# State scan of a two-direction GRU: three columns an image with prepared operands, in place of four

## The reference

```
def step(h, xt):
    gh = h @ whh.T + bhh
    xr, xz, xn = jnp.split(xt, 3, axis=-1)
    hr, hz, hn = jnp.split(gh, 3, axis=-1)
    r = jax.nn.sigmoid(xr + hr)
    z = jax.nn.sigmoid(xz + hz)
    n = jnp.tanh(xn + r * hn)
    h_new = (1.0 - z) * n + z * h
    return (h_new, h_new)
...
yf = _gru_dir(z @ gru_wih_f.T + gru_bih_f, gru_whh_f, gru_bhh_f, False)
yb = _gru_dir(z @ gru_wih_b.T + gru_bih_b, gru_whh_b, gru_bhh_b, True)
y = jnp.concatenate([yf, yb], axis=-1) @ out_w.T + out_b
return x + y.reshape(Bx, Hx, Wx, C)
```

## Time and profile before

| | us |
|---|---|
| median of 3 runs | 1848.66 |
| lowest, highest | 1848.02, 1849.30 |
| the profiled execution | 1848.42 |
| its span, from the first to the last instruction | 1846.6 |
| TensorE, VectorE, ScalarE busy | 1639.6, 1578.8, 1227.9 |

### The profile page before, as it was taken

The page is one execution under the profiler, slowest core; times in us unless marked ns, Lnnn a source line. Parts: engine busy times, 40 slices in busy tenths (PEclk is TensorE's granted clock), DMA queues, the critical chain, the costliest instruction groups (busy, mean ns, idle before and its releaser), DMA issues.

```text
span 1846.6 us, 65131 instructions
## 1 busy us (share of the span) xinstructions
PE 1639.6 (89%) x21315; PEld 1240.3 (67%) x21315; DVE 1578.8 (85%) x9056; ACT 1227.9 (66%) x6271; POOL 58.2 (3%) x131
## 2 busy tenths in 40 slices
PE   3558999999999999999999999999999999999997
PEld 2436777676777777777777777776777777777775
DVE  7879888888888888888888888888888888888887
ACT  7935666666666666666666666666666666666665
POOL 5520000000000000000000000000000000000000
PEclk9655555555555555555555555555555555555555
DMA  5200000000000000000000000000000000000000
GB/s 157 69 7 8 13 11 14 11 14 11 13 11 12 12 11 14 10 14 11 13 11 8 11 14 11 12 12 12 12 12 12 11 14 11 13 11 12 12 12 15
DMA packets 40132, 31.27 MB, mean 17 GB/s; under 512 B 3448, under 2 KB 37624, under 8 KB 39800
## 3 DMA queue, kind: packets, MB, share of 16 engines
q1 hardware_dynamic: 39800, 27.13, 5.1%
HBM read 18.73 MB, written 8.39 MB: 15 GB/s over the span
## 4 chain that ended last, share of the span: by engine, by line
PE 56%; DVE 22%; ACT 14%; issue 7%; DMA 0%; POOL 0%; SPq 0%; DVEq 0%; ACTq 0%; POOLq 0%
PE bank L592 56%; DVE state L888 8%; DVE bank L876 8%; ACT rec L496 7%; DVE halves L897 4%; ACT rpair L490 3%; ACT big L432 2%; ACT seq L428 1%; ACT xin L416 1%; DMA gamma_row<-in_gamma 0%; DVE seq L851 0%; DVE rec L903 0%; DVE big L867 0%; ACT zquad L493 0%; DVE xin L821 0%
## 5 line engine op out<-in xcount | busy, mean ns | idle before, releaser
L592 PEld LDWEIGHTS bank<-halves,wsplit 128*128 128x128 f16 x18432 | 697.8, 106 | 504.4 <-DVE halves L897 376.7
L592 PE MATMUL bank<-halves,wsplit 128*128 128x16 f16 x18432 | 883.6, 182 | 133.2 <-DVE halves L897 118.6
L888 DVE TENSOR_TENSOR_SCAN state<-zquad,rec 128x64 f32<-128x64 f32 x2048 | 596.2, 291 | 177.0 <-ACT rec L496 135.1
L592 PE MATMUL bank<-seq,wcomb 128*128 128x128 f32 x1536 | 593.0, 491 | 0.4 <-DVE seq L851 0.4
L496 ACT ACTIVATE rec<-bank 128x16 f32<-128x16 f32 x2048 | 406.5, 198 | 276.4 <-DVE bank L876 81.4
L490 ACT ACTIVATE rpair<-bank 128x16 f32<-128x16 f32 x2048 | 378.9, 185 | 285.7 <-PE bank L592 267.9
L897 DVE SCALAR_TENSOR_TENSOR halves<-state 128x32 f16<-128x32 f32 x2048 | 433.1, 211 | 34.8
L876 DVE TENSOR_TENSOR_SCAN bank<-rpair,bank 128x32 f32<-128x32 f32 x2048 | 440.5, 215 | 22.3 <-ACT rpair L490 6.2
L493 ACT ACTIVATE zquad<-bank 128x16 f32<-128x16 f32 x2048 | 407.6, 199 | 25.1
L592 PEld LDWEIGHTS bank<-seq,wcomb 128*128 128x128 f32 x1536 | 385.9, 312 | 1.3 <-DVE seq L851 1.3
L903 DVE TENSOR_TENSOR rec<-state,signs 128x32 f32<-128x32 f32 x2047 | 370.9, 181 | 3.0
(11 more groups left out here) (118 smaller groups left out, 204.8 us busy)
## 6 DMA issues: line engine op xcount, KB each, us to landing
xin<-in_x SPq DMA_DIRECT2D x16, 512.0 KB, 3.7
big<-in_x SPq DMA_DIRECT2D x128, 64.0 KB
out<-big SPq DMA_DIRECT2D x128, 64.0 KB
wih<-in_wiht SPq DMA_DIRECT2D x2, 384.0 KB
con<-in_consts SPq DMA_DIRECT2D x1, 424.0 KB, 5.3
whh<-in_whht SPq DMA_DIRECT2D x2, 192.0 KB
inw<-in_in_w SPq DMA_DIRECT2D x1, 128.0 KB
outw<-in_outwt SPq DMA_DIRECT2D x2, 64.0 KB
```

The costliest lines, as they stand in the source:

```text
L592: return nc.tensor.matmul(o, w, m, start=start, stop=True, skip_group_check=True)
L888: v.tensor_tensor_scan(state[:, d, ring, :], zquad[:, e, cols], rec[:, e, cols], 0.0, ALU.mult, ALU.add).then_inc(state_ready[d], 1)
```

## The change

The state scan has three columns an image. Its first operand, `gain`, holds 0, K * (1 - z), 1; its second, `drive`, holds -n, (1 - z - 1) * h, -BIG, and is subtracted. The columns become n, K * (1 - z) * n + z * h, which is the new state, and the new state + BIG. ScalarE writes 1 - z to a dense tile `keep` and tanh of the negated candidate to column 0 of `drive`. VectorE makes the middle columns: `scale_gain` multiplies `keep` by K into `gain`, and `hold_state` computes (`keep` - 1) * h, with the last state h, into `drive`. Both are of 16 columns. They stand in `body` where `record_state` stood, but belong to the state scan that follows them, of the same direction and step. `signs`, `rec`, `zquad` and `rec_ready` go; `gain_ready` and `drive_ready` come. The memsets of the start are 11 in place of 15. The split, the projection and `state_of` read every third column where they read every fourth.

```diff
--- before
+++ after
-    state = sb("state", [P, 2, RING + 1, 4 * B])
-    rec = sb("rec", [P, 2, 4 * COLS])
-    signs = sb("signs", [P, 2 * COLS])
+    state = sb("state", [P, 2, RING + 1, 3 * B])
+    drive = sb("drive", [P, 2, 3 * COLS])
-    zquad = sb("zquad", [P, 2, 4 * COLS])
+    keep = sb("keep", [P, 2, COLS])
+    gain = sb("gain", [P, 2, 3 * COLS])
...
                     act.wait_ge(update_pre[d], turn)
-                    act.activation(zquad[:, e, 4 * B * d:4 * B * (d + 1)].rearrange("p (n k) -> p n k", k=4)[:, :, 2],
+                    act.activation(keep[:, e, B * d:B * (d + 1)],
                                    Z[q][:, at:at + B], ACT.Sigmoid, scale=negative).then_inc(update_ready[d], 1)
                     act.wait_ge(cand_pre[d], turn)
-                    act.activation(rec[:, e, 4 * B * d:4 * B * (d + 1)].rearrange("p (n k) -> p n k", k=4)[:, :, 0],
+                    act.activation(thirds_of(drive, e, d)[:, :, 0],
...
-                                   ACT.Tanh, scale=inverse).then_inc(cand_ready[d], 1)
+                                   ACT.Tanh, scale=negative).then_inc(cand_ready[d], 1)
...
             dve.wait_ge(cand_ready[d], turn)
-            dve.wait_ge(update_ready[d], turn)
-            if not (isinstance(base, int) and base + r == 0):
-                dve.wait_ge(rec_ready[d], base + r)
-            v.tensor_tensor_scan(state[:, d, ring, :], zquad[:, e, cols], rec[:, e, cols], 0.0,
-                                 ALU.mult, ALU.add).then_inc(state_ready[d], 1)
+            dve.wait_ge(gain_ready[d], turn)
+            if turn > 1:
+                dve.wait_ge(drive_ready[d], turn - 1)
+            v.tensor_tensor_scan(state[:, d, ring, :], gain[:, e, cols], drive[:, e, cols], 0.0,
+                                 ALU.mult, ALU.subtract).then_inc(state_ready[d], 1)
...
-        def record_state(r, d):
+        def scale_gain(base, r, d):
             e = r % 2
-            new = state_of(r, d)
-            v.tensor_tensor(rec[:, 1 - e, 4 * B * d:4 * B * (d + 1)].rearrange("p (n k) -> p n k", k=4)[:, :, 1:3],
-                            new[:, :, 2:3].to_broadcast([P, B, 2]),
-                            signs[:, 0:2 * B].rearrange("p (n k) -> p n k", k=2), ALU.mult).then_inc(rec_ready[d], 1)
+            dve.wait_ge(update_ready[d], base + (r + 1))
+            v.tensor_scalar(thirds_of(gain, e, d)[:, :, 1], keep[:, e, B * d:B * (d + 1)], K, None,
+                            ALU.mult).then_inc(gain_ready[d], 1)
+
+        def hold_state(base, r, d):
+            e = r % 2
+            old = state_of((r - 1) % RING, d)
+            v.scalar_tensor_tensor(out=thirds_of(drive, e, d)[:, :, 1], in0=keep[:, e, B * d:B * (d + 1)], scalar=-1.0,
+                                   in1=old[:, :, 1], op0=ALU.add, op1=ALU.mult).then_inc(drive_ready[d], 1)
...
                 candidate(base, r, 0)
-                if not (first and r == 0):
-                    record_state((r - 1) % RING, 1)
+                scale_gain(base, r, 0)
+                if base + r > 0:
+                    hold_state(base, r, 0)
...
                 new_state(base, r, 0)
                 candidate(base, r, 1)
                 split_state(base, r, 0)
-                record_state(r, 0)
+                scale_gain(base, r, 1)
+                if base + r > 0:
+                    hold_state(base, r, 1)
                 new_state(base, r, 1)
                 split_state(base, r, 1)
```

More of the change, by code:

```diff
@@ L230, in build @@
     halves_ready = [sem(f"halves_ready{d}") for d in range(2)]
-    rec_ready = [sem(f"rec_ready{d}") for d in range(2)]
+    gain_ready = [sem(f"gain_ready{d}") for d in range(2)]
+    drive_ready = [sem(f"drive_ready{d}") for d in range(2)]
     square_set = sem("square_set")
@@ L260, in state_of, with thirds_of @@
     def state_of(r, d):
-        return state[:, d, r // TB * TB + place(r % TB, d), :].rearrange("p (n k) -> p n k", k=4)
+        return state[:, d, r // TB * TB + place(r % TB, d), :].rearrange("p (n k) -> p n k", k=3)
+    def thirds_of(t, e, d):
+        return t[:, e, 3 * B * d:3 * B * (d + 1)].rearrange("p (n k) -> p n k", k=3)
     block = ctx.enter_context(nc.Block())
@@ L332, in _ @@
         sp.wait_ge(out_done, 16 * NBLK)
-    N_INIT = 15
+    N_INIT = 11
     @block.gpsimd
@@ L340, in _ @@
         for e in range(2):
[L341 to L350, removed]
+            thirds = gain[:, e, :].rearrange("p (n k) -> p n k", k=3)
+            g.memset(thirds[:, :, 0], 0.0).then_inc(init_done, 1)
+            g.memset(thirds[:, :, 2], 1.0).then_inc(init_done, 1)
+            thirds = drive[:, e, :].rearrange("p (n k) -> p n k", k=3)
+            g.memset(thirds[:, :, 1], 0.0).then_inc(init_done, 1)
+            g.memset(thirds[:, :, 2], -BIG).then_inc(init_done, 1)
         g.memset(halves[:, :, :, :, :], 0.0).then_inc(init_done, 1)
@@ L622, in project @@
         def project(q, d):
-            h = state[:, d, q * TB:(q + 1) * TB, :].rearrange("p s (b k) -> p (s b) k", k=4)[:, :, 2]
+            h = state[:, d, q * TB:(q + 1) * TB, :].rearrange("p s (b k) -> p (s b) k", k=3)[:, :, 1]
             return mm(Y[:, d * C:(d + 1) * C], h, outw[:, d, :], start=(d == 0))
@@ L880, in new_state @@
         def new_state(base, r, d):
-            e, cols = r % 2, slice(4 * B * d, 4 * B * (d + 1))
+            e, cols = r % 2, slice(3 * B * d, 3 * B * (d + 1))
             ring = r // TB * TB + place(r % TB, d)
@@ L895, in split_state @@
             slot = r // TB * TB + place(r % TB, d)
-            both = state[:, d, slot::RING - slot, 2::4]
-            v.scalar_tensor_tensor(out=halves[:, e, d, :, :], in0=new[:, :, 3].unsqueeze(1).to_broadcast([P, 2, B]),
+            both = state[:, d, slot::RING - slot, 1::3]
+            v.scalar_tensor_tensor(out=halves[:, e, d, :, :], in0=new[:, :, 2].unsqueeze(1).to_broadcast([P, 2, B]),
                                    scalar=-BIG, in1=both, op0=ALU.add, op1=ALU.subtract).then_inc(halves_ready[d], 1)
-        def record_state(r, d):
+        def scale_gain(base, r, d):
             e = r % 2
-            new = state_of(r, d)
-            v.tensor_tensor(rec[:, 1 - e, 4 * B * d:4 * B * (d + 1)].rearrange("p (n k) -> p n k", k=4)[:, :, 1:3],
-                            new[:, :, 2:3].to_broadcast([P, B, 2]),
-                            signs[:, 0:2 * B].rearrange("p (n k) -> p n k", k=2), ALU.mult).then_inc(rec_ready[d], 1)
+            dve.wait_ge(update_ready[d], base + (r + 1))
[6 more added lines that the diff above has]
+                                   in1=old[:, :, 1], op0=ALU.add, op1=ALU.mult).then_inc(drive_ready[d], 1)
         def body(base, kblk, first):
```

## The result

The changed kernel takes 1918.26 us (median of 4 runs, 1916.40 to 1919.51) against 1848.79: a ratio of 1.0376, 95% interval 1.0361 to 1.0392. It is 69.5 us slower. The forecast was 1854 with a range to 1876. The profiled execution is 1917.26 us, its span 1915.4.

What follows compares the result with a forecast made beforehand. VectorE's order and latency in a ring through both directions bound 768 steps, TensorE's bias fill 256. Ring -1.5, output addition +10, ScalarE's outputs -3.6 make +5 on 1848.7: 1854 us, range 1836 to 1876.

Steps and rivals of the forecast that it cites:

- The ring: Loop of scans and splits through both directions on VectorE: 1.62 us a plain step before, 1.618 forecast, in 768 steps.
- S1: Backward state scan: before, tanh and recording said to end together ahead of it; after, the hold releases it.
- The 256 steps held by the strided bias fill: Two of eight steps, bound by TensorE at 1.80 and 1.76 us; expected to stay unchanged.
- Multiply and hold, backward half: Between forward split and backward state scan: 0.13 + 0.08 + 0.175 + 0.035 = 0.42 us in place of 0.35.
- H1: Backward split, 0.33 us after the backward state scan before the change, 0.04 of it hand-over; 0.294 in the forecast.
- Forward half: Multiply and hold between forward candidate scan and state scan: hidden behind tanh, 0.04 us to spare, in 512 steps.
- S0: Forward state scan: released by tanh, except 0.04 us late in the 256 output-addition steps.
- C0: Forward candidate scan, start of the loop; the forward state scan follows 0.49 us later, with tanh between.
- Output addition: Forward half, 256 steps: the addition now follows the hold, starting the state scan 0.04 us late; +10 us (0 to 28).
- Rival 1: Small VectorE instructions are cheap and tanh still decides: 1831 us, centre of the case 1838; chance 0.33.
- Rival 3: Output addition holds VectorE for its whole 0.27 us, forward state scan 0.11 late in 256 steps: 1872 us; chance 0.08.
- Rival 4: Each added VectorE instruction costs its full length, delaying hold and output addition: about 1990 us; chance 0.02.

Runs made afterwards that it cites:

- Experiments 1 to 4: State scan's waits: hold's first in the changed kernel (1880.01 us), backward only (1855.88); opposite order in the kernel before (2015.54); changed kernel with one semaphore (1823.40).
- experiment 8: Kernel before with one wait per state scan, plus already-met waits ahead of each recording (1847.33 us), then also ahead of each split (1850.92 us).
- experiment 3: Kernel before with its three waits ahead of the state scan in the opposite order: 2015.54 us, ratio 1.0894.
- experiment 1: Changed kernel with the hold's wait written first in both directions, so that the state scan itself carries it: 1880.01 us, ratio 1.0161.

## Why the prediction was wrong

**What bounds the kernel: right, but for one reading.** The ring through both directions and VectorE's order explains the kernel before, the changed one and the one with one wait; without the multiply a single direction's ring takes over. S1 did not have two reasons to start where it does: in the kernel before it starts 0.033 after tanh's end in nearly every step, as in the forward half, and the recording's end holds nothing, since what it writes is for the next step. The 256 steps held by the strided bias fill stay nearly out of it. Two such in a row take 3.51 us after (median; one pair of forward splits is at 718.97 and 722.49) against 3.56 before, some 7 us in all, which the prediction put at nothing.

**State scan: right,** 33 ns, at the lower end. Against the 36 in the sum that is 0.006 a ring step, 5 us.

**Multiply and hold, backward half: the step that failed.** Their slots and durations came out as taken (0.077 and 0.175), but "the hand-over to S1 by semaphore is the one from S1 to H1 ... I take 0.035" was read from an instruction with one wait. S1 has three. The hand-over was 0.132, 0.097 more than the term in the sum. The ring in place of 1.618 is 1.701, against 1.617 before, and 0.084 x 768 = +64 us. Experiments 1 to 4 show that it is this term: with the wait put on the scan, or with one wait, the hold's start to S1 is 0.21 to 0.24.

**The point was visible.** The prediction said that S1 now waits for what is written directly ahead of it, and named the hold as its releaser, but not which of S1's waits sits in the scan. The order of the three lines in `new_state` decides that, and the trace of before had the extra instruction at L887.

**Forward half: not hidden, but cheap.** The prediction had the hold and its hand-over done 0.04 ahead of S0. With 0.132 in place of 0.035 the hold releases S0 too, in nearly every step: S0 starts 0.132 after its end and 0.047 after tanh's, where tanh alone needs 0.033. So C0 to S0 is 0.50 against 0.49. With one wait tanh releases S0, and it is 0.48.

**Output addition: the mechanism wasn't at work here.** Hold to addition 0.09 and addition to S0 0.22 (725.37 to 725.59) make the 0.31 that the hand-over takes anyway, so it cost nothing more. In the kernel with one wait its slot shows, 0.20 as taken, and costs 0.02 and not 0.04 in 256 steps.

**ScalarE's outputs: right and without effect.** The dense update gate takes 184 ns, as taken. The 3.6 us that this was to save in the output steps are not there, since those steps lost nothing that it could give back.

**Instruction supply: undersized.** The prediction says of the instructions added that "whatever instruction fetch costs is within the bounds": the pauses cost 24.1 us against 12.9, so +11. The ledger is then 64 - 7 + 11 = 68, and 69.5 was measured.

**The rivals.** Rival 1, small instructions cheap and a faster kernel, is nearest to what the change does once its waits are put right: 1823, below the 1838 I gave it. Its mechanism holds by half: tanh decides S0 then, but the hold, 0.035 before it, decides S1. Rival 3 is refuted in the changed kernel, where S0 starts 0.22 and not 0.27 after the addition. Rival 4, the full length of each instruction, is refuted: the hold starts 0.08 after a multiply of 0.17. The Trainium skill's rule that the next op waits for an empty pipe ("VectorE: DVE Perf Modes", section The DRAIN you can't avoid) does not hold for these instructions in this trace either; the same section adds that a next op that is not held starts earlier, which the prediction left out and the trace agrees with. The sign of the forecast was right by luck: it rested on the output addition's 10 us, which never came, and left out the 0.10 of the hand-over.

## What to carry to other kernels

An instruction that waits for several semaphores is two instructions: its own wait costs nothing beyond the hand-over, one in the separate instruction 0.05 or 0.1 us more if it comes last. So count the waits of the instruction at the end of each link, find which one comes last, and put that one on the instruction itself, or let all the producers count up one semaphore. When a change adds a dependency right ahead of its reader, look at that before judging the idea: here the same change is 3.8% slower, 0.4% slower or 1.4% faster by how its waits are written, and 2.8% faster once its multiply is folded away. And count the instructions of a long unrolled loop, semaphore instructions too: the pauses on VectorE came at each 128th here, and what one cost depended on where it fell.

## What the runs showed of the hardware that was not expected

- A separate semaphore instruction with two waits shows 49 to 50 ns once it is the bottleneck and adds about 0.10 us from the last producer's end to the reader's start (0.132 against 0.035); with one wait it shows 21 ns (candidate scan's line, and the recording's in experiment 8).
- Which of its two waits is met last matters: from tanh's end to the scan it is 0.130 where tanh's wait is the second (experiment 3) and 0.087 where it is the first (experiment 1, forward half). This was read off the traces, not tested by itself.
- Semaphore instructions that never wait still cost: two a step more raised the ratio to the kernel before from 0.9965 to 0.9989, two more to 1.0013, 4.4 us each time, with the ring unchanged.
- The pauses of VectorE that make a step long lie at each 128th instruction recorded on it, in all twelve kernels, and go with one packet of the instruction queue q14 for each 128.
